# A graph-attention pass: the last pair of gathered tiles is scaled on ScalarE, head by head, instead of on VectorE

## The reference, cut to what matters

```python
h = (x @ W).reshape(N, H, C)                      # H = 4 heads of C = 64
e = leaky_relu(a_src[src] + a_dst[dst], 0.2)      # per edge and head
p = exp(e - m[dst])
out = segment_sum(alpha[:, :, None] * h[src], dst)   # alpha = p / sum of p
```

## Time and profile before

| | us |
|---|---|
| median of 3 runs | 7864.47 (7858.81 to 7873.66) |
| the profiled execution: its time | 7869.87 |
| the profiled execution: its span | 7868.1 |
| busy: PE, PEld | 5554.7 (71%), 4678.6 (59%) |
| busy: DVE | 3895.8 (50%) |
| busy: ACT | 1587.9 (20%) |
| busy: POOL | 5661.0 (72%) |

### The profile page before, as it was taken

How to read it: one execution, slowest core, us unless ns; L and a number is a source line. 1 busy time by engine, 2 the same in 40 slices (tenths; PEclk the granted TensorE clock), 3 DMA queues, 4 the chain that set the end, 5 groups by cost and what they waited for, 6 DMA issues and landing times. The chain is left out here.

```text
span 7868.1 us, 110058 instructions
## 1 busy us (share of the span) xinstructions
PE 5554.7 (71%) x27644; PEld 4678.6 (59%) x27645; DVE 3895.8 (50%) x10085; ACT 1587.9 (20%) x3574; POOL 5661.0 (72%) x6057
## 2 busy tenths in 40 slices
PE   3888888888883698992455555555555689999993
PEld 3666666666663588881344334333434589999983
DVE  4777777888888400004454444444444633333326
ACT  1222222222220333330000000000000234444441
POOL 3777777777776677776677777777777767777762
PEclk7888888888885799996777777777777879988886
DMA  3333333333334244444333333333332123333698
GB/s 120 105 105 105 106 105 102 98 97 96 97 96 124 97 155 153 154 155 116 110 105 97 93 93 92 93 92 93 92 93 81 26 71 81 79 80 78 76 71 184
DMA packets 428345, 799.53 MB, mean 102 GB/s; under 512 B 129927, under 2 KB 267899, under 8 KB 427982
## 3 DMA queue, kind: packets, MB, share of 16 engines
q0 software_dynamic: 237808, 481.17, 27.0%
q1 hardware_dynamic: 190430, 317.21, 12.0%
HBM read 726.97 MB, written 70.98 MB: 101 GB/s over the span
## 5 line engine op out<-in xcount | busy, mean ns | idle before, releaser
L1048 PE MATMUL g_pM<-g_G,g_S 128*128 128x256 f32 x3328 | 1219.3, 545 | 1264.4 <-DMA g_G<-table,g_IDX 1232.8
L746 POOL DMA_INDIRECT g_G<-table,g_STG x1664 | 1658.9, 997 | 478.3 <-issue 445.6
L760 POOL DMA_INDIRECT g_G<-table,g_IDX x1664 | 1584.6, 952 | 537.9 <-issue 506.0
L1048 PEld LDWEIGHTS g_pM<-g_G,g_S 128*128 128x128 f32 x3328 | 934.4, 288 | 1549.4 <-issue 1295.9
L1018 PE MATMUL g_pM<-g_G,g_S 128*128 128x260 f32 x3328 | 1122.6, 476 | 388.3 <-DVE acc L861 378.1
L601 POOL DMA_INDIRECT slots<-sort_PAIR,sort_ADDR x1024 | 1043.7, 1019 | 379.9 <-issue 310.9
L1591 POOL DMA_INDIRECT q_G<-table,slot x1072 | 1027.1, 958 | 362.2 <-issue 322.7
L869 DVE TENSOR_TENSOR acc<-g_pM,acc 128x256 f32 x1664 | 697.5, 419 | 1109.9 <-PE g_pM L1048 1107.0
L1018 PEld LDWEIGHTS g_pM<-g_G,g_S 128*128 128x128 f32 x3328 | 689.5, 227 | 677.1 <-DVE acc L861 562.0
L861 DVE TENSOR_TENSOR acc<-g_pM,acc 128x260 f32 x1664 | 710.6, 427 | 167.9 <-PE g_pM L1018 24.2
L849 DVE TENSOR_SCALAR g_S<-iota,g_REL,g_WT 128x128 f32<-128x128 f32 x1664 | 583.4, 351 | 189.7 <-issue 172.7
(11 more groups left out here) (322 smaller groups left out, 7264.5 us busy)
## 6 DMA issues: line engine op xcount, KB each, us to landing
e_W<-in_L_ffn_W SPq DMA_DIRECT2D x210, 512.0 KB
sort_PAIR<-slot_rows SPq DMA_DIRECT2D x66, 512.0 KB, 4.7
g_G<-table,g_STG POOLq DMA_INDIRECT x1664
g_G<-table,g_IDX POOLq DMA_INDIRECT x1664
ys_all<-ew_Y SPq DMA_DIRECT2D x196, 128.0 KB, 1.7
sm_Y<-ys_all SPq DMA_DIRECT2D x28, 896.0 KB
q_ST<-slot_rows SPq DMA_DIRECT2D x34, 512.0 KB, 3.9
sort_ADDR<-slot_rows SPq DMA_DIRECT2D x34, 512.0 KB
```

The source lines that it names most:

```text
L746: pool.indirect_dma_start(G[:, r, u, :], None, table, bass.IndirectOffsetOnAxis(ap=STG[:, r, u:u + 1].bitcast(U32), axis=0)).then_inc(gath ...
L760: pool.indirect_dma_start(G[:, r, u, :], None, table, bass.IndirectOffsetOnAxis(ap=IDX[:, k * GRP + u:k * GRP + u + 1].bitcast(U32), axis= ...
L1048: m = pe.matmul(pM[r % 2 * 2 + half][:, u % HG, :], S[:, r, u, :], G[:, r, u, :], start=True, stop=True)
```

## The change

The fourth product of each group leaves DVE. ACT multiplies the last two tiles in eight activations of 64 columns, one for each tile and head, in place in G, with the factor read from the column of G that the second exponential has just written. They stand behind the copy of the next group's one-hots and ahead of the sort's two activations. PE waits for a new semaphore, `gp_scalar`, before pair sum 3, and `gp` now counts three products in a group.

```diff
-        names += ["staged", "slots_free", "iota", "part", "copied", "z", "lr", "arg", "p", "pcol", "gp"]
+        names += ["staged", "slots_free", "iota", "part", "copied", "z", "lr", "arg", "p", "pcol", "gp", "gp_scalar"]
...
                 product(2)
-                product(3)
                 if phase == "rank" and r % 2 == 1:
                     keep_ranks(b, r // 2)
...
+                def last_pair(k, r):
+
+                    a.wait_ge(s["pcol"], k + 1)
+                    for u in range(GRP - 2, GRP):
+                        for h in range(HEADS):
+                            head = G[:, r, u, h * (D // HEADS):(h + 1) * (D // HEADS)]
+                            m = a.activation(head, head, ACT.Copy, scale=G[:, r, u, D + h:D + h + 1])
+                    m.then_inc(s["gp_scalar"], 1)
...
-                    at_least(a, s["gp"], k * HG)
+                    at_least(a, s["gp"], k * (PAIRS - 1))
                     a.activation(factors(r % 2), ARG[:, r % 2], ACT.Exp).then_inc(s["p"], 1)
                     a.activation(G[:, r, :, D:D + HEADS], ARG[:, r % 2], ACT.Exp).then_inc(s["pcol"], 1)
                     if not last(rnd, r):
                         copy(k + 1)
+                    last_pair(k, r)
...
-                pe.wait_ge(s["gp"], k * PAIRS + pair + 1)
+                if pair < PAIRS - 1:
+                    pe.wait_ge(s["gp"], k * (PAIRS - 1) + pair + 1)
+                else:
+                    pe.wait_ge(s["gp_scalar"], k + 1)
```

## The result

| | before | after |
|---|---|---|
| median | 7864.95 us (7 runs) | 7894.76 us (7 runs) |
| ratio | | 1.0036, 95% interval 1.0025 to 1.0047 |
| profiled span | 7868.1 | 7891.5 |
| busy DVE, ACT, POOL | 3895.8, 1587.9, 5661.0 | 3774.5, 1983.7, 5680.7 |

The forecast was 7890.5. DVE has 121 us less to do, the kernel takes 30 us more.

What follows compares the result with a forecast made beforehand. POOL bounds the count phase and, after the change, the rank phase at 22.59 us per two groups instead of the DVE-PE cycle's 22.16. Terms +21.1, +5.1 and -0.6 give +26 on 7864.47, 7890.5 us; range 7859 to 7902.

Steps and rivals of the forecast that it cites:

- Product 3 is slack: Count and rank phases: removing DVE's 0.60 us product per group only lengthens its waits for DMA or PE, gain 0.
- ACT's work costs nothing: Eight activations ahead of the sort's two take 1.85 us, ending 2.3 us before ACT must be free: cost 0.
- The copy catches the gather 0.06 us behind it: Rank phase: the predicated copy, starting 0.60 us sooner, makes that gather lose 1.11 us instead of 0.45.
- POOL becomes the bound: Rank phase: POOL needs 22.59 us for two groups, more than the 22.16 of the DVE-PE cycle; chance 0.60.
- The scan's share: Rank phase: POOL's loss per two groups to gathers held by the scan, 1.25 us, last gather 0.9 behind it.
- least distance: Rank phase: DVE falls back until Z comes 1.82 us after the group's last gather ends.
- The rest: POOL's time for two rank groups without losses to scan and copy, taken from the count phase: 20.23 us.
- the 49 intervals: Between the rank phase's 50 scans: 49 x (22.59 - 22.16) = +21.1 us.
- End of the phase: Last scan step's Z to the last Z: four groups take 46.2 us instead of 41.1, +5.1 us.
- the address operations: End of rank phase: POOL, ahead of them before, now meets these DVE operations and loses 3.4 us in one group.
- The sum: Whole kernel: +21.1, +5.1 and -0.6 give +26 us, 7890.5 against the median, 0.33% slower.
- the likeliest case's range: Whole kernel, gather caught and POOL bound: +6 to +38 us, 7870 to 7902, with scan loss 0.86 to 1.6.

Runs made afterwards that it cites:

- e5: Changed kernel plus three idle DVE operations of 128 columns ahead of the predicated copy in scan steps, copy 0.60 us later: 7866.01 us, ratio 0.9992.
- e6: Changed kernel plus one idle DVE operation of 128 columns ahead of the predicated copy in scan steps, copy 0.20 us later: 7870.87 us, ratio 1.0001.
- e7: Changed kernel plus one idle DVE operation of 32 columns ahead of the predicated copy in scan steps, copy 0.10 us later: 7873.79 us, ratio 1.0002.
- e2: Changed kernel without the eight activations and PE's wait for them, last two tiles summed unmultiplied: 7891.86 us, ratio 1.0029.
- e3: Kernel before, all four products on DVE, plus eight idle activations of 64 columns on ACT: 7869.49 us, ratio 1.0003.
- e1: Kernel before, all four products on DVE, with the predicated copy ahead of product 3 in scan steps: 7900.49 us, ratio 1.0038.
- e12: Changed kernel with the scan behind product 1 and, in scan steps, the predicated copy behind the next step's one-hots: 7841.77 us, ratio 0.9948.
- e8: Changed kernel with the scan behind product 1 instead of ahead of product 0: 7858.42 us, ratio 0.9984.
- e11: Kernel before, all four products on DVE, with the scan behind product 1: 7897.09 us, ratio 1.0019.
- e4: Changed kernel with the predicated copy ahead of product 2 in scan steps: 7875.60 us, ratio 1.0010.

## Why the prediction was right, point by point

- **Product 3 is slack.** Held. The count phase kept its 713 to 714 gathers in 900 us, and e5, e6 and e7, where the copy no longer does harm and product 3 is still off DVE in all 208 groups, are at 0.9992 to 1.0002: nothing gained.
- **ACT's work costs nothing.** Held, by e2 and e3. Its size was 2.00 us, not 1.85. The estimate of 1.9 by the Trainium skill ("ScalarE: Activation LUTs", What ACT_TABLE_LOAD costs) is nearer.
- **The copy catches the gather 0.06 us behind it.** Held: 1.12 us against the 1.11 forecast, in all 50 pairs. e1 shows that this place alone makes the whole difference, and e5, e6 and e7 that 0.1 to 0.6 us more distance takes it away. The rule of the Trainium skill ("SBUF — State Buffer", Who interferes with whom) that whoever starts first has the pair gave the same answer here, but e7's gather 0.01 us behind the copy went through, so the measurement decides.
- **POOL becomes the bound.** Held, with two terms mis-sized in opposite ways. The pace is 22.66, not 22.59. The scan's share is 1.41 us and not 1.25: `Z` comes later than its least distance of 1.82 us behind the last gather, 1.94 in the 32 scan steps where the DMA releases it and 2.38 in the 18 where PE does, and POOL's gather then starts 0.73 us behind the scan in the mean and not 0.9. The rest is 20.13 and not 20.23. That the sum came within 0.07 is partly luck. That PE still ends most of `Z`'s idle time in the rank phase (113.6 of 175.2 us) was not forecast. Of the 49 intervals comes (22.66 - 22.16) x 49 = +24.5 us for +21.1.
- **End of the phase.** The size held, +4.5 us for +5.1, but by luck. The last scan step's `Z` is at 2380.4 - 2.67 = 2377.7 and the last `Z` at 2423.3, 45.6 us for four groups instead of 41.1. The forecast took POOL to be ahead of the address operations before and to lose 3.4 us to them now. The timelines of POOL show that it meets them in both kernels and loses the same 0.9 us, some 0.45 on the stage copy and 0.42 on the gather behind it. Before:

```profile
2363.93 1.46 POOL L746 DMA_INDIRECT g_G<-table,g_STG  x1 [0.31 <-issue]
2365.40 0.65 POOL L736 COPY g_STG<-X 128x8 int32<-128x8 int32 x1
2366.21 1.37 POOL L746 DMA_INDIRECT g_G<-table,g_STG  x1 [0.16 <-POOL g_STG L736]
```

After:

```profile
2386.27 2.11 POOL L746 DMA_INDIRECT g_G<-table,g_STG  x1 [0.30 <-issue]
...
2388.38 0.66 POOL L736 COPY g_STG<-X 128x8 int32<-128x8 int32 x1
...
2389.20 1.37 POOL L746 DMA_INDIRECT g_G<-table,g_STG  x1 [0.16 <-POOL g_STG L736]
```

What did change is POOL's lead: four groups of gathers lie behind the last scan step's `Z` where three did before. The forecast's 2.5 us too much for the address operations were nearly made up by the last `Z`, which came 3.9 us after the last gather (it had ended at 2419.4) and not 2.
- **The sum.** The last `Z` moved by 28.1 us (24.5 + 4.5 less 1.0 that the first scan came sooner) and the medians by 29.8; the forecast was 26. The profiled span moved by 23.4 only: behind the pass the profiled execution after is 4.7 us shorter than the one before. What gave this is open. The top of the likeliest case's range, +38, is the 49 intervals alone, (20.23 + 1.6 + 1.11 - 22.16) x 49; with the forecast's other terms it would be +43.

## What to carry to other kernels

Taking work off an engine with slack moves everything behind it, and an operation that locks out GpSimd can then start just ahead of a gather instead of just behind: 0.6 us of slack bought a loss of 0.7 us a pair. Where POOL issues gathers back to back, read the timeline of POOL beside the DVE operations with two SBUF inputs and add the held time per period; a few tenths of idle work or another order (e12: 0.5% faster) is worth more than the work saved. Moving a long operation off the path between two engines that wait for each other is half of it: with the scan behind product 1 the pace was 21.93 us a pair where POOL lost 0.58 us to the copy (e8), and 22.34, worse than the 22.16 before, where it lost 1.14 (e11).

## What the runs showed of the hardware

- The edge is sharp and differs by operation. In the timelines of the kernels before, after and e1, e4 to e8, e11 and e12, all gathers that started up to 0.02 us behind a predicated copy went through (23 starts from 0.00 to 0.02), all from 0.04 to 0.14 us were held (123), and at 0.03 three went and two were held. Behind the scan 10 starts from 0.05 to 0.08 us went through, and all 17 from 0.09 to 0.15 were held. In the trace's nanoseconds, which the timelines round, the last start behind the copy that went through is at 34 and the first that was held at 36; behind the scan they are at 79 and 93.
- A gather that is held ends 0.75 to 0.78 us after the scan does, or 0.77 to 0.85 us after the predicated copy. One under way is not stopped: in e6 gathers that had started 0.05 to 0.09 us ahead of the copy took their 0.94 to 0.97 us.
- POOL's stage copy of eight columns is held too, 1.36 us instead of 0.20 in e11, but its edge and its end are others: in e11 it was held also where it started up to 0.01 us ahead of the predicated copy, and it ends within 0.03 us of the end of the operation that held it in all the runs listed.
